# Storing the finished high and low halves of weight pieces and down weights in DRAM for the second pair of blocks, on one core

## What is computed

```
x = x + softmax(layernorm-like(sim(layernorm(x), ctx)))      # 4 blocks of 512 x 512
y = layernorm(x)
weights = router(y)                                          # per token, 8 experts
gate[e] = y @ Wg[e] (+ y @ Ga[e] @ Gb[e] for e = 0, 1)       # 512 x 512 each
up[e]   = y @ Wu[e] (+ y @ Ua[e] @ Ub[e] for e = 0, 1)
mid[e]  = silu(gate[e]) * up[e]
out[e]  = mid[e] @ Wd[e] (+ mid[e] @ Da[e] @ Db[e] for e = 0, 1)
x = x + sum over e of weights[e] * out[e]
```

## Time and profile before

| | |
|---|---|
| median of 3 runs | 1072.06 us (1071.26 to 1073.39) |
| the profiled execution, its own time | 1073.63 us |
| its span, first to last instruction | 1071.9 us |
| TensorE (PE) busy | 1045.8 us, 98% |
| VectorE (DVE) busy | 755.6 us, 70% |
| ScalarE (ACT) busy | 443.2 us, 41% |
| GpSimd (POOL) busy | 54.7 us, 5% |
| moved by DMA | 94.74 MB, mean 88 GB/s |
| mean granted TensorE clock | 0.997 |

### The profile page before, as it was taken

The page is one execution under the profiler, slowest core; times in us unless marked ns, Lnnn a source line. Parts: engine busy times, 40 slices in busy tenths (PEclk is TensorE's granted clock), DMA queues, the critical chain, the costliest instruction groups (busy, mean ns, idle before and its releaser), DMA issues.

```text
span 1071.9 us, 12318 instructions
## 1 busy us (share of the span) xinstructions
PE 1045.8 (98%) x4680; PEld 854.1 (80%) x4680; DVE 755.6 (70%) x1278; ACT 443.2 (41%) x631; POOL 54.7 (5%) x60
## 2 busy tenths in 40 slices
PE   6899999999999999999999899999999999999998
PEld 4687878877888888888888788788888888888887
DVE  6889688968485775859487695857658484847654
ACT  4453342555253344435334344534434442524430
POOL 1711122100000000000000010000000000000000
PEclk9999999999999999999999999999999999999999
DMA  9401104145141231514125354311121121111112
GB/s 316 129 15 36 79 9 169 49 129 157 42 142 51 93 108 59 157 60 136 42 98 177 118 157 165 111 40 60 40 79 40 60 60 35 64 39 64 35 40 79
DMA packets 88140, 94.74 MB, mean 88 GB/s; under 512 B 4368, under 2 KB 61840, under 8 KB 87184
## 3 DMA queue, kind: packets, MB, share of 16 engines
q1 hardware_dynamic: 86928, 90.73, 26.5%
q0 software_dynamic: 864, 3.15, 1.0%
q10 hardware_dynamic: 288, 0.07, 0.0%
HBM read 76.63 MB, written 17.30 MB: 88 GB/s over the span
## 4 chain that ended last, share of the span: by engine, by line
PE 80%; DVE 12%; issue 4%; DMA 3%; ACT 1%; SPq 0%; POOL 0%; DVEq 0%
PE gate_up L1557 13%; PE gate_up L1559 13%; PE gate_up L1558 13%; PE tiles L1447 10%; PE tiles L1448 10%; PE tiles L1449 10%; PE gate_up L1515 2%; PE gate_up L1516 2%; PE gate_up L1521 2%; DVE piece_lo L1110 2%; DVE mids_lo L1188 2%; DVE mids L1156 1%; DVE wd_lo L1118 1%; DVE lora_w L1089 1%; PE tiles L1480 1%
## 5 line engine op out<-in xcount | busy, mean ns | idle before, releaser
L1557 PE MATMUL gate_up<-xT_hi,piece_hi 128*128 128x512 f32 x448 | 174.7, 390 | 2.5 <-DVE piece_lo L1110 2.5
L1447 PE MATMUL tiles<-wd_hi,mids_hi 128*128 128x512 f32 x448 | 174.7, 390 | 0.5 <-DVE mids_lo L1188 0.5
L1449 PE MATMUL tiles<-wd_hi,mids_lo 128*128 128x512 f32 x448 | 174.5, 390 | 0.0
L1448 PE MATMUL tiles<-wd_lo,mids_hi 128*128 128x512 f32 x448 | 174.5, 390 | 0.0
L1559 PE MATMUL gate_up<-xT_lo,piece_hi 128*128 128x512 f32 x448 | 174.3, 389 | 0.0
L1558 PE MATMUL gate_up<-xT_hi,piece_lo 128*128 128x512 f32 x448 | 174.3, 389 | 0.0
L1162 DVE SCALAR_TENSOR_TENSOR xacc<-tiles,rw,xacc 128x512 f32<-128x512 f32 x112 | 78.0, 750 | 127.3 <-PE tiles L1449 127.3
L1110 DVE TENSOR_TENSOR piece_lo<-piece,piece_hi 128x1024 fp32r<-128x1024 f32 x112 | 118.1, 1096 | 27.9 <-ACT piece_hi L739 27.9
L1557 PE MATMUL gate_up<-tx_hi,piece_hi 128*128 128x512 f32 x336 | 132.0, 393 | 3.4 <-DVE gates L1143 2.8
L1559 PE MATMUL gate_up<-tx_lo,piece_hi 128*128 128x512 f32 x336 | 131.3, 391 | 0.0
L1558 PE MATMUL gate_up<-tx_hi,piece_lo 128*128 128x512 f32 x336 | 131.3, 391 | 0.0
(11 more groups left out here) (166 smaller groups left out, 1448.7 us busy)
## 6 DMA issues: line engine op xcount, KB each, us to landing
piece<-in_wg_dram SPq DMA_DIRECT2D x40, 256.0 KB, 3.2
piece<-in_wu_dram SPq DMA_DIRECT2D x40, 256.0 KB, 3.4
wd_raw<-in_wd_dram SPq DMA_DIRECT2D x10, 1024.0 KB, 5.1
piece<-merged SPq DMA_DIRECT2D x32, 256.0 KB, 3.2
merged<-lora_w SPq DMA_DIRECT2D x6, 1024.0 KB, 4.2
x_back<-x_spill SPq DMA_DIRECT2D x9, 512.0 KB, 5.3
w_raw<-in_xT_dram SPq DMA_DIRECT2D x4, 1024.0 KB, 6.2
wd_raw<-merged SPq DMA_DIRECT2D x4, 1024.0 KB, 5.6
```

The source lines that it names most:

```text
L1447: nc.tensor.matmul(dst, w_h, x_h, start=first, stop=False)
L1448: nc.tensor.matmul(dst, w_h, x_l, start=False, stop=False)
L1449: return nc.tensor.matmul(dst, w_l, x_h, start=False, stop=last)
L1557: nc.tensor.matmul(dst, w_h, x_h, start=first and kt == 0, stop=False, skip_group_check=True)
```

## The change

SP now stores the finished halves of each of the 28 pieces of steps 0 to 6 (`piece_hi` and slots 1 to 7 of `piece_lo`, 7 KB a partition each) to a DRAM tensor `piece_spill`, and those of the seven down weights (`wd_hi`, `wd_lo`, 8 KB a partition each) to `wd_spill`. In steps 7 to 13 it loads these halves straight into `piece_hi`, `piece_lo`, `wd_hi` and `wd_lo`; the sums and splits on VectorE and ScalarE are left out there, and TensorE waits for the loads. The store of piece j - 2 is issued just before the load of piece j, and that load also waits until the store of piece j - 3 is complete, since it writes the same buffer. The store of down weights k - 1 stands before the load of down weights k, which waits for it.

```
         x21_spill = nc.dram_tensor("x21_spill", [P, 2 * S], fp32, kind="Internal").ap()
+        piece_spill = nc.dram_tensor("piece_spill", [4 * SWAP, 2, P, 7 * 2 * P], fp32, kind="Internal").ap()
+        wd_spill = nc.dram_tensor("wd_spill", [SWAP, 2, P, FT * D], fp32, kind="Internal").ap()
...
+            def store_piece(j):
+                sp.wait_ge(piece_ready[j % 3], j // 3 + 1)
+                for part, halves in enumerate((piece_hi[j % 3][:, :, :], piece_lo[j % 3][:, 1:8, :])):
+                    sp.dma_start(piece_spill[j, part, :, :].rearrange("p (g c) -> p g c", g=7), plain(halves))\
+                      .then_inc(piece_stored[j % 3], 16)
+
+            def load_piece_back(j):
+                for part, halves in enumerate((piece_hi[j % 3][:, :, :], piece_lo[j % 3][:, 1:8, :])):
+                    sp.dma_start(plain(halves), piece_spill[j - 4 * SWAP, part, :, :].rearrange("p (g c) -> p g c", g=7))\
+                      .then_inc(piece_back[j % 3], 16)
+
             def load_next_piece(j):
                 if j < 4 * STEPS:
+                    if 2 <= j < 4 * SWAP + 2:
+                        store_piece(j - 2)
                     sp.wait_ge(p_mm[4], j - 2)
-                    load_piece(j)
+                    if j - 3 < 4 * SWAP:
+                        sp.wait_ge(piece_stored[j % 3], 32 * (j // 3))
+                    if j < 4 * SWAP:
+                        load_piece(j)
+                    else:
+                        load_piece_back(j)
+
+            def store_wd(k):
+                sp.wait_ge(wd_ready, k + 1)
+                for part, halves in enumerate((wd_hi, wd_lo)):
+                    sp.dma_start(wd_spill[k, part, :, :].rearrange("p (f d) -> p f d", f=FT), plain(halves[:, :, :])).then_inc(wd_stored, 16)
+
+            def load_wd_back(k):
+                for part, halves in enumerate((wd_hi, wd_lo)):
+                    sp.dma_start(plain(halves[:, :, :]), wd_spill[k - SWAP, part, :, :].rearrange("p (f d) -> p f d", f=FT)).then_inc(wd_back, 16)
...
             load_lora_factors(0)
+            store_piece(0)
             load_next_piece(3)
...
                 if k != SWAP:
                     load_next_piece(4 * k + 4)
+                if k <= SWAP:
+                    store_wd(k - 1)
                 sp.wait_ge(d_mm, 8 * k)
-                load_wd(k)
+                if k <= SWAP:
+                    sp.wait_ge(wd_stored, 32 * k)
+                if k < SWAP:
+                    load_wd(k)
+                else:
+                    load_wd_back(k)
...
             def piece_high_part(j):
-                if j < 4 * STEPS:
+                if j < 4 * SWAP:
...
             def wd_high_part(k):
+                if k >= SWAP:
+                    return
...
             def piece_sums(j):
-                if j >= 4 * STEPS:
+                if j >= 4 * SWAP:
                     return
...
             def piece_low_part(j):
-                if j >= 4 * STEPS:
+                if j >= 4 * SWAP:
                     return
...
             def wd_low_part(k):
+                if k >= SWAP:
+                    return
...
-                pe.wait_ge(piece_ready[j % 3], j // 3 + 1)
+                if j < 4 * SWAP:
+                    pe.wait_ge(piece_ready[j % 3], j // 3 + 1)
+                else:
+                    pe.wait_ge(piece_back[j % 3], 32 * ((j - 4 * SWAP) // 3 + 1))
...
-                pe.wait_ge(wd_ready, k + 1)
+                if k < SWAP:
+                    pe.wait_ge(wd_ready, k + 1)
+                else:
+                    pe.wait_ge(wd_back, 32 * (k - SWAP + 1))
```

More of the change, by code:

```diff
@@ L278, in xattn_ffn_kernel @@
         piece_ready = [sem(f"piece_ready{i}") for i in range(3)]
+        piece_stored = [sem(f"piece_stored{i}") for i in range(3)]
+        piece_back = [sem(f"piece_back{i}") for i in range(3)]
+        wd_stored = sem("wd_stored")
+        wd_back = sem("wd_back")
         wd_loaded = sem("wd_loaded")
```

## The result

The changed kernel takes 1090.68 us (median of 4 runs), the kernel before 1071.66: 19.0 us or 1.8% more by the medians. The ratio of the means is 1.0192 with a 95% interval of 1.0141 to 1.0243; it is the larger of the two because one of the four executions took 1099.07 us. The direction was forecast, the size was not: +7.3 was forecast, and the measured time lies at the very end of the range. The profiled execution took 1089.89 us, with a span of 1088.3; its distance to the profiled execution of before is 16.3 us, so nearly 3 us of the difference between the medians lie in executions that no trace here shows.

What follows compares the result with a forecast made beforehand. The second pair of blocks was taken to be bound by TensorE, with added stores delaying loads on SP's queue. Terms 4.2 + 0 + 4.3 - 1.2 = +7.3 us on the median 1072.06 gave 1079.4 us, range 1073.5 to 1091.

Steps and rivals of the forecast that it cites:

- Term 1: Start of the first pair (k = 0): piece 3's load comes late behind the stores of pieces 0 and 1; TensorE stalls +4.2 us.
- Term 2: Steps k = 1 to 5: load delays swallowed by VectorE's idle time; down weights cost 0, upper bound 1 us a step.
- Term 3: Step k = 6: a store delays piece 26's load, without cover; the chain and TensorE move by +4.3 us.
- Term 4: Second pair: sums and splits leave VectorE and ScalarE; TensorE gets back waits of 0.5 and 0.7 us, -1.2 us.
- Rival A: Stores of steps 0 to 6 are slow or confirmed late (300 GB/s, 6.1 us each): +23, 1095 us; chance 0.22.
- Rival B: Loads at k = 0 and 6 not held up by stores issued ahead: 1069.9 to 1071.4 us; chance 0.10.

## Why the prediction was right or wrong

**What bounds the kernel: right.** The second pair stayed at 266 matmuls in 60 us, though VectorE's work there fell from 39 to 24 us and ScalarE's to 17.

**Term 1, +4.2: mechanism right, size 4.9.** The load of piece 3 landed at 234.5 where I had 233.3, and the stall before low_rank was 5.7 us (I said near 5). The stores began later than counted: the older transfers were not through at 221.6, as the rate in 221 to 223 shows, and the end of store 1 was slow (columns as in rows 2):

```profile
222.00:223.00 1.00, 1.00 (x6) 0.81 (x6) 0.47 (x1) 1.00 (x1) 0.00 (x0) 1.00 1.10 293
231.00:232.00 1.00, 1.00 (x6) 0.82 (x5) 0.00 (x0) 0.22 (x1) 0.00 (x0) 1.00 0.98 208
```

In between they ran as counted (430 GB/s in 224 to 226). Store 0 was confirmed at 227.9 instead of 226.4, and SP issued the load then, but that was not what the load waited for: store 1, ahead of it in the queue, landed only at 232.8, and the load 1.7 us behind it. The 0.5 us that I gave a store's semaphore came from no row.

**Term 2, steps 1 to 5, 0: wrong, +3.0 in the trace.** This is the step that failed. The delay of piece 4k + 2 was as forecast (VectorE waits 4.57 us at 334.18, near the 4.3 to 5) and was swallowed. What failed is the sentence on down weights, "so they meet. Cost 0". From the issue of the piece's load to the confirmation of the store behind it I counted 8.1 us (345.47 to 353.6); it took 9.3 (351.32 to 360.6), and 9.2 in the kernel that stores down weights only. So the confirmation came 1.2 us after TensorE's release. And I had not counted the piece's store behind the load, with which the load itself took 1.3 us longer. My upper bound of 1 us a step held; 0.6 was measured. The same error, in the two places where the queue is fuller, made the next two terms wrong. With the store of down weights issued earlier, and nothing else changed, the kernel took 9.2 us less. In the traces, 3.0 us here, 3.1 in step 6 and 0.9 at piece 32 are 7 of the 9 us that the sum lacks.

**Term 3, +4.3: 3.8 for the stall, right; but step 6 lost 4 us more.** The sentence that "that cost is paid already" failed for the clock: TensorE ran at 1.2 GHz for 5.5 us after the stall instead of 3.8, which cost 1.0 us more; I had allowed 1 to 2 for it, outside the sum. And as much as in steps 1 to 5 together was lost once more, in no term at all: in step 6 the store of down weights 5 stands behind the store of piece 26 and the load of piece 28, which is now 1.8 MB of finished halves instead of 0.5 MB, and its second half, issued at 611.82, is confirmed only 12.9 us later, when SP issues the next load at 624.79. ScalarE, in order, is held 6.8 us in front of the high parts of mids and of the copy `s_sb`, and TensorE stalls 2.7 us for that copy, 3.1 with what follows. I had bounded this wait at 1 us a step from a step without x_back loads, and did not work it out for the one step whose queue is full.

**Term 4, -1.2: not gained.** The wait of 0.5 us at the swap went, but TensorE waited 1.6 us for piece 32 instead of saving its 0.7. I had named this place as tight, with up to 2 us to lose; in the run with the early store it is gone.

**Rival A** (1084 to 1095) holds the measured time, and its sign, TensorE waiting in steps 2 to 5, came true. Half of its cause did too: a store was confirmed late. The other half did not: the stores were not slow, they ran at the 426 GB/s of the row, and its late gates in those steps did not come. By the rule of the Trainium skill that I had weighed against it (DMA: Bandwidth & Descriptors, Where 436 GB/s comes from: some 358 GB/s from the HBM side) they would have taken an estimated 5.1 us; the window with 430 GB/s of stores sides with the row. **Rival B** is excluded: pieces 3 and 26 came late.

## What to carry to other kernels

Time saved on an engine that TensorE doesn't wait for is worth nothing, and the transfers that buy it are free only where nobody waits for the next one. Before adding a store to a queue, go through every transfer behind it and its own completion, in the fullest step and not in the typical one, and ask how much room the consumer has; rooms that cover each delay alone don't cover the sum. A second queue alone was no remedy here: it freed the loads and slowed the store whose confirmation the next load waits for. And before a gain of 0.2% is read off two traces, look where each traced execution lies among the runs of its kernel.

## What the runs showed of the hardware

A load is slowed by a store that is issued behind it on the same queue. The 1 MB of down weights, on idle DMA engines, landed in 5.1 to 5.5 us (median 5.4, down weights only) and 4.9 to 5.7 (median 5.2, before) with nothing right behind it, and in 6.3 to 7.0 (median 6.7, changed kernel) and 6.3 to 6.9 (median 6.6, pieces only) with a piece's store of 1.8 MB right behind it. The store's data did not get in between: in 361 to 366 us of the changed kernel 0.91 MB were moved, in 446 packets, 2 KB each, as the load's rows are. The engines moved it at 200 to 234 GB/s where it had been 397 before the change. What holds it is not shown.

Size over rate is too short for a chain that ends with a confirmation. From the issue of a piece's load to the confirmation of the store of down weights behind it (0.5 and 2.1 MB, an estimated 6.2 us at the 426 GB/s of rows 5) passed 9.2 us in the kernel with down weights only and 9.3 in the changed kernel.

A stall can bring a second price, the clock. In the changed kernel the granted clock was 0.50 in these windows (columns as in rows 2):

```profile
242.00:244.00 2.00, 2.00 (x6) 1.52 (x6) 2.00 (x5) 0.00 (x0) 0.00 (x0) 0.50 0.14 57
604.00:606.00 2.00, 0.00 (x0) 0.00 (x0) 2.00 (x4) 1.23 (x2) 0.00 (x0) 0.50 0.74 164
610.00:612.00 2.00, 2.00 (x6) 1.52 (x6) 1.89 (x2) 0.60 (x1) 0.00 (x0) 0.50 1.02 430
```

In step 6 TensorE stood still for 6.7 us, the clock fell within it, and came back 5.5 us after the first matmul. In the trace of before it fell just after TensorE resumed from the stall of 2.8 us and came back 3.8 us after the first matmul. That cost 1.6 us: the kernel with down weights only, which had no fall, was 0.4 us ahead at the first matmul after the stall and 2.0 ahead 13 matmuls later (598.01 against 599.99). The price does not follow from the stall's length: after stalls of 1.6 to 2.1 us the clock did not fall, nor after the one of 2.7 us in the changed kernel, though it did with one of 2.7 us, for piece 32, in the kernel with the second queue. And after stalls of 8.3 us (pieces 0 and 1 not stored) and 9.2 us (load ahead of the store) it was back 3.3 and 3.1 us after the first matmul, sooner than after 6.7. In step 0 the 4.0 us at 1.2 GHz after low_rank had begun cost little, as forecast, because TensorE would have waited for low halves there anyway.
